# A graph layer on one core: look-ups in the order of their PSUM banks, masks bank by bank, layer one in two parts

## The reference

```python
h = maximum(layernorm(x), 0)                    # x: 12500 nodes x 32
e = concatenate([h[src], h[dst], edge_attr])    # 400000 edges, sorted by dst
hid = relu(e @ W1 + b1)                         # 96 -> 64
v = hid @ W2 + b2                               # 64 -> 32
out = x + maximum(segment_max(v, dst, 12500), h)
```

## Time and profile before

| what | us |
| --- | --- |
| measured, median of 3 runs | 3184.88 |
| lowest and highest | 3180.12 and 3187.65 |
| span of the profiled execution | 4798.8 |
| TensorE busy in it | 3796.5 |
| GpSimd busy in it | 2386.6 |
| ScalarE busy in it | 2192.4 |
| VectorE busy in it | 2178.1 |

### The profile page before, as it was taken

The page is one execution under the profiler, slowest core; times in us unless marked ns, Lnnn a source line. Parts: engine busy times, 40 slices in busy tenths (PEclk is TensorE's granted clock), DMA queues, the critical chain, the costliest instruction groups (busy, mean ns, idle before and its releaser), DMA issues.

```text
span 4798.8 us, 56874 instructions
## 1 busy us (share of the span) xinstructions
PE 3796.5 (79%) x19778; PEld 2547.3 (53%) x19778; DVE 2178.1 (45%) x2474; ACT 2192.4 (46%) x2555; POOL 2386.6 (50%) x2523
## 2 busy tenths in 40 slices
PE   5858788778878877877887788778877887778787
PEld 3536455555555545555555555555555555555465
DVE  4211554445444444544444455444444454445356
ACT  2214454445444444544444445444544454445355
POOL 6653455555455455455545555555455555554310
PEclk8979888888778888888887888888888888888798
DMA  8700222222222222222222222222222222222112
GB/s 255 279 10 25 70 80 88 92 85 61 57 68 63 56 66 69 56 61 68 68 55 63 68 65 61 60 69 68 56 63 68 69 61 56 68 68 68 46 55 56
DMA packets 200553, 350.32 MB, mean 73 GB/s; under 512 B 73791, under 2 KB 124251, under 8 KB 200117
## 3 DMA queue, kind: packets, MB, share of 16 engines
q1 hardware_dynamic: 116638, 303.65, 18.4%
q0 software_dynamic: 80448, 41.33, 6.2%
q10 hardware_dynamic: 3332, 4.01, 0.3%
HBM read 240.36 MB, written 119.78 MB: 75 GB/s over the span
## 4 chain that ended last, share of the span: by engine, by line
PE 60%; issue 19%; another core or an unknown queue 10%; DVE 8%; ACT 2%; DMA 0%; DVEq 0%; ACTq 0%; SPq 0%
PE ps_rows L938 38%; PE ps_layers L968 8%; PE ps_layers L963 5%; DVE onehot L1250 3%; PE ps_layers L918 2%; PE ps_layers L953 2%; PE ps_layers L912 2%; DVE max_t L1318 2%; PE ps_layers L957 2%; PE ps_layers L1006 1%; DVE src_t L1285 1%; DVE rows_in L1323 1%; ACT onehot L852 0%; DVE dst_t L1305 0%
## 5 line engine op out<-in xcount | busy, mean ns | idle before, releaser
L664 POOL DMA_INDIRECT src_in<-h_dram,src_ix x2269 | 2147.7, 947 | 1951.5 <-PE ps_rows L938 976.5
L938 PE MATMUL ps_rows<-onehot,table 128*128 128x512 f32 x9898 | 2553.2, 418 | 109.0 <-issue 89.3
L938 PEld LDWEIGHTS ps_rows<-onehot,table 128*128 128x128 f32 x9898 | 1986.6, 203 | 728.8 <-issue 292.8
L852 ACT ACTIVATE onehot<-distance 128x1024 fp32r<-128x1024 bf16 x909 | 905.0, 1049 | 855.0 <-PE ps_rows L938 607.3
L847 ACT ACTIVATE distance<-picks,below_column 128x1024 bf16<-128x1024 int16 x909 | 985.1, 1139 | 0.7 <-DMA picks<-picks_dram 0.7
L838 ACT ACTIVATE hid<-ps_layers,b_col 128x512 f32<-128x512 f32 (+1 forms) x404 | 241.6, 680 | 1407.9 <-remote 912.0
L1300 DVE STREAM_TRANSPOSE ps_layers<-rows_in 128x512 f32<-128x512 f32 x202 | 133.3, 706 | 1561.3 <-ACT hid L838 1561.2
L968 PE MATMUL ps_layers<-picked_rows,w_src 128*64 128x128 f32 x1552 | 399.9, 390 | 550.1 <-issue 545.7
L1250 DVE SCALAR_TENSOR_TENSOR onehot<-picks,column,ps_layers 128x1024 fp32r<-128x1024 int16 x404 | 499.8, 1258 | 310.2 <-PE ps_rows L938 164.7
L968 PEld LDWEIGHTS ps_layers<-picked_rows,w_src 128*64 128x64 f32 x1552 | 188.8, 180 | 784.9 <-issue 782.2
L1318 DVE TENSOR_TENSOR_SCAN max_t<-mask_in,max_t,ps_layers 128x512 f32<-128x512 bf16 x196 | 249.0, 1271 | 337.2 <-remote 331.4
(11 more groups left out here) (145 smaller groups left out, 1283.1 us busy)
## 6 DMA issues: line engine op xcount, KB each, us to landing
picks<-picks_dram SPq DMA_DIRECT2D x101, 512.0 KB
first_rows<-hid SPq DMA_DIRECT2D x100, 500.0 KB
rows_in<-in_edge_attr_dram SPq DMA_DIRECT2D x96, 512.0 KB
rows_in<-first_rows SPq DMA_DIRECT2D x96, 512.0 KB
run_max<-rows_in SPq DMA_DIRECT2D x96, 512.0 KB
src_in<-h_dram,src_ix POOLq DMA_INDIRECT x2269
mask_in<-mask_dram SPq DMA_DIRECT2D x96, 256.0 KB
h_dram<-h_sb ACTq DMA_DIRECT2D x4, 392.0 KB, 5.9
```

The lines of the kernel that those rows point to most:

```text
L664: pool.indirect_dma_start(out=src_in[:, slot, g, r, :], out_offset=None, in_=rows[:, :], in_offset=bass.IndirectOffsetOnAxis(ap=src_ix[:, ...
L852: nc.scalar.activation(onehot[:, RING_AT[c] + BY_DVE[c] + k, :, :].rearrange("p g w -> p (g w)"), distance[:, k, :], ACT.Relu, bias=1.0, s ...
L938: mm = nc.tensor.matmul(ps_rows[g][side][:, 0:WIDE], table[:, i * SIDES + side, part, :], onehot[:, RING_AT[c] + t, g, :], start=(i + part ...
```

## The change

Four things are written otherwise; the arithmetic is the same.

1. The look-ups of a chunk go bank by bank, in the order (side 1, g 0), (side 1, g 1), (side 0, g 0), (side 0, g 1), where before each tile went over sides and parts with g innermost. A new semaphore `banks_summed` counts the first three banks of the last chunk, and `tiles_used` goes up at the ends of banks (by 3 at the end of the last chunk).
2. Each of the four operations of `mask_rows` waits for its own bank, and each bank of chunk 0 waits for the mask that read it.
3. Layer one stands in two parts: edges and dst rows, two banks of chunk 0, gathered and picked rows, the other two banks of chunk 0. Layer two moves behind chunk 1.
4. VectorE's order in a pair is now: one-hot of chunk 0, masks, turn_edges, turn_src, (a wait for `hid` of pair j), one-hot of chunk 2, fill_dst, find_side, one-hot of chunk 3, find_max.

```diff
-                    for side in range(SIDES if i < WIDE_TILES else 1):
-                        last_tile = TILES - 1 if side == 0 else WIDE_TILES - 1
-                        parts = PARTS if i < WIDE_TILES else 1
-                        for part in range(parts):
-                            for g in range(2):
-                                mm = nc.tensor.matmul(ps_rows[g][side][:, 0:WIDE], table[:, i * SIDES + side, part, :],
+                    if side and i >= WIDE_TILES:
+                        continue
+                    last_tile = WIDE_TILES - 1 if side else TILES - 1
+                    parts = PARTS if i < WIDE_TILES else 1
+                    for part in range(parts):
+                        mm = nc.tensor.matmul(ps_rows[g][side][:, 0:WIDE], table[:, i * SIDES + side, part, :],
...
+                if c == CHUNKS - 1:
+                    if n < len(BANKS) - 1:
+                        mm.then_inc(banks_summed, 1)
+                    else:
+                        mm.then_inc(tiles_used, CHUNK[c])
+                elif n >= len(BANKS) - CHUNK[c]:
                     mm.then_inc(tiles_used, 1)
...
-                    layer_one(j, slot, True, short)
-                look_up(j + 2, slot, 0)
+                    layer_edges(j, slot)
+                    layer_dst(j, slot)
+                    look_up_bank(j + 2, 0, 0)
+                    look_up_bank(j + 2, 0, 1)
+                    layer_src(j, short)
+                    layer_picks(j, slot, short)
+                    look_up_bank(j + 2, 0, 2)
+                    look_up_bank(j + 2, 0, 3)
+                look_up(j + 2, 1)
...
-                dve.wait_ge(tiles_used, j * TILES + WIDE_TILES)
                 for g in range(2):
+                    dve.wait_ge(banks_summed, j * (len(BANKS) - 1) + (g + 1))
...
+                turn_src(j + 1, (k + 1) % (2 * AHEAD), turn + (k + 1) // (2 * AHEAD))
+                dve.wait_ge(hid_made, j * A + A)
+                dve.sem_inc(layer_passed, 1)
+                one_hot(j + 2, slot, 2)
                 fill_dst(j + 1, 1 - slot, of_next * D + D, of_next * D + D, j + 1)
-                one_hot(j + 2, slot, 2)
+                find_side(j + 2, slot)
+                one_hot(j + 2, slot, 3)
                 find_max(j, slot, stored)
-                one_hot(j + 2, slot, 3)
-                find_side(j + 2, slot)
-                turn_src(j + 1, (k + 1) % (2 * AHEAD), turn + (k + 1) // (2 * AHEAD))
```

More of the change, by code:

```diff
@@ L922, in _, with look_up_bank @@
             pe.wait_ge(table_step, TABLE_STEPS)
[L924 to L927, removed]
+            def look_up_bank(j, c, n):
+                side, g = BANKS[n]
+                if c == 0 and (not isinstance(j, int) or j > 0):
+                    if side:
+                        pe.wait_ge(second_side, j * 2 - 1 + g)
+                    else:
+                        pe.wait_ge(rows_masked, j * MASKS - 1 + g)
+                if n == 0 and BY_DVE[c]:
@@ new lines, in look_up_bank @@
+                    last_tile = WIDE_TILES - 1 if side else TILES - 1
+                    parts = PARTS if i < WIDE_TILES else 1
+                    for part in range(parts):
+                        mm = nc.tensor.matmul(ps_rows[g][side][:, 0:WIDE], table[:, i * SIDES + side, part, :],
+                                              onehot[:, RING_AT[c] + t, g, :],
+                                              start=(i + part == 0), stop=(i == last_tile and part == parts - 1))
+                if c == CHUNKS - 1:
+                    if n < len(BANKS) - 1:
+                        mm.then_inc(banks_summed, 1)
+                    else:
+                        mm.then_inc(tiles_used, CHUNK[c])
+                elif n >= len(BANKS) - CHUNK[c]:
@@ L941, in look_up, with layer_edges @@
                     mm.then_inc(tiles_used, 1)
-            def layer_one(j, slot, ahead=True, short=False):
+            def look_up(j, c):
+                for n in range(len(BANKS)):
+                    look_up_bank(j, c, n)
+            def layer_edges(j, slot):
                 wait(pe, max_scanned, j * 2)
-                pe.wait_ge(onehot_made, j * DVE_ALL + (2 * DVE_ALL + 1 if ahead else (PAIRS - j) * DVE_ALL))
-                pe.wait_ge(side_found, j + 2 if ahead else PAIRS)
-                pe.wait_ge(dst_filled, j * 2 + 2 if ahead else PAIRS * 2)
+                pe.wait_ge(onehot_made, j * DVE_ALL + (2 * DVE_ALL + 1))
+                pe.wait_ge(side_found, j + 2)
+                pe.wait_ge(dst_filled, j * 2 + 2)
@@ L1019, in pair @@
                     layer_two(j)
-                for c in range(1, CHUNKS):
-                    look_up(j + 2, slot, c)
+                for c in range(2, CHUNKS):
+                    look_up(j + 2, c)
             for j in range(2):
                 for c in range(CHUNKS):
-                    look_up(j, j, c)
+                    look_up(j, c)
             for j in range(2):
@@ L1291, in turn_edges, with fill_dst @@
                     V.transpose(of_half(ea_t[:, slot, :, :], h), ea_in[:, slot, h, :, :]).then_inc(ea_turned, 1)
-            def fill_dst(j, slot, loaded, masks, through, columns=(BLK, BLK), before=(BLK, BLK)):
+            def fill_dst(j, slot, loaded, masks, through, columns=(BLK, BLK), before=(BLK, BLK), made=True):
                 dve.wait_ge(first_loaded[slot], loaded)
@@ L1410, in _ @@
             turn_edges(0, 0, D)
-            fill_dst(0, 0, D, D, 0)
+            fill_dst(0, 0, D, D, 0, made=False)
             def pair(j, k, turn, stored, before_last=False):
@@ L1443, in tail_pair @@
                     dve.wait_ge(side_found, PAIRS)
[L1444 to L1446 removed]
+                    fill_dst(j + 2, slot, moved_up_to(j + 2), ((j + 2) // 2 + 1) * D, j + 1, columns_of(j + 2), columns_of(j + 1), made=False)
             for k in range(2 * AHEAD):
```

38 lines of the change are left out of this document (25 added, 13 removed).

## The result

The changed kernel takes 3199.87 us (3198.63 to 3201.24), the kernel before 3186.27 us in the same comparison: a ratio of 1.0045, 95% interval 1.0032 to 1.0059. So it is slower by 14 us. The forecast of 3186 us, "within 0.2%", was not what came. The time lies inside the range, but that is luck in part: the range had been widened upwards for rival B, in which TensorE sets the time, and what came is not B, as the experiments show.

A forecast was written before the change was run, and what follows sets the result against it. GpSimd's issuing of gathers was taken to bound the kernel, 30.04 against TensorE's 27.28 us a pair. The terms 3184.9 + 0 + 1 (the end) + 0 gave 3186 us, range 3170 to 3228 for 8 in 10.

The forecast's parts named there:

- rival B: Whole kernel: TensorE sets the time, split runs add 33 us; 3218 us (3205 to 3228), chance 0.24.
- What bounds the kernel: Main loop: GpSimd's issuing of gathers sets the time, 30.04 us a pair against TensorE's 27.28.
- Its sum for GpSimd: Rebuilt unprofiled time: 352 to the loop's start, 2812 for 2247 gathers, 12 behind the last; 3176 us.
- TensorE's own sum: Rebuilt unprofiled time by TensorE: start at 359, pairs 2619, the end 115.5; 3094 us, 91 below the median.
- 96 pairs of 27.28: TensorE's main loop: every pair at the undisturbed pace of 27.28 us, 2619 us in all.
- The split: TensorE's pair: one more look-up run and layer restart, 0.34 us (0.2 to 0.44), 33 us in all, covered by gathers.
- The bank order: TensorE's look-ups, now in runs into one bank: no change taken from 0.227 us each.
- a lead of 91: TensorE against the measured time: its sum of 3094 us stood 91 us below the median.
- The end: Behind the last gathers: longer VectorE latency paid once, 17.5 + 96.0 = 113.5 against GpSimd's 113.9; 0 to 3 us, 1 taken.
- T + 17.5: Last pair: its edges start 17.5 us after the last gathers land, instead of some 5.
- C: Rival, program's end: latency behind the last landing is dearer, masks or find_max 5 to 10 us late; 3190 to 3195, chance 0.08.
- The start: First gathers of the loop: earlier turn_src can save between 0 and 10 us; 0 taken.

The follow-up runs named there:

- second profile of before: The kernel before, unchanged, run once more for a profile without the first profile's gaps; span 3180.4 us, against 4798.8 us in the first.
- Experiment 6: The kernel before with one gather of rows in 24 left out, the last of each pair from 7 to 95; 3152.31 us, 0.9907 of before.
- experiment 1: The kernel before with VectorE's new order alone; look-ups, masks and layer one as before; 3198.36 us, 1.0051 of before.
- the last run of experiment 5: The changed kernel with turn_src behind find_max in pairs 90 to 95 and SLACK 13 for 6; 3182.55 us, 1.0002 of before.
- experiment 4: The changed kernel with turn_src behind find_max in all pairs, 3203.51 us; then also with SLACK 13 for 6, 3203.84 us.
- the run of experiment 3: The changed kernel with turn_src alone moved behind find_max in the last 15 pairs (from 84 on); 3189.90 us, 1.0022 of before.

## Why the prediction was right and wrong

**What bounds the kernel: right.** Its sum for GpSimd was 352 + 2812 + 12 = 3176. In the second profile of before the loop's first gather starts at 357.3, the last of all at 3168.6, 2811 later, and 11.8 us follow. That 2812 met 2811 so closely is luck: the step is 1.2486 us and not 1.2515, 6.5 us less over 2247 steps, and 5.14 of waiting for the stores and 2.0 of gaps, which the sum did not have, make up for it. 1.25 us from gather to gather holds in the profile that isn't stretched, with the same 0.30 between windows that the prediction's sentence on the Trainium skill (Perfetto Trace Analysis, "Per-instruction lifecycle: what the profiler-reported window actually captures") rested on. Experiment 6 shows the rest.

**TensorE's own sum: mis-sized.** It was 3094; experiment 6, in which TensorE ends last, has 3152. The term that failed is "96 pairs of 27.28". In experiment 6, and in the kernel before too, the first 13 pairs took 388 us and not 355; in that stretch one-hots wait for the loads of `picks`, as ScalarE's row of before has it:

```profile
ACT distance L847 <- DMA picks<-picks_dram: 72.1, 11, 8.7
```

Another 14 us of experiment 6 are in pairs 27, 28, 41, 42, 55, 69 and 70, that is every 14 pairs, the length of VectorE's loop.

The longest stretch of before, pairs 82 and 83, is not TensorE's own. TensorE's rows, VectorE's fill_dst in the same pair, and SyncE's waits from 2640 to 2700 us:

```profile
2683.30 11.15 PE L938 MATMUL ps_rows<-onehot,table 128*128 128x512 f32 x42 [11.91 <-DVE onehot L1250]
...
2700.26 2.02 PE L953 MATMUL ps_layers<-ea_t,w_edge 32*64 32x512 f32 x16 [5.81 <-DVE onehot L1250]
```

```profile
2678.12 1.32 DVE L1300 STREAM_TRANSPOSE ps_layers<-rows_in 128x512 f32<-128x512 f32 x2 [20.06 <-DMA mask_in<-mask_dram]
```

```profile
SPq L607 <- DMA src_in<-h_dram,src_ix: 38.3, 2, 23.3
```

SyncE waits at line 607 for GpSimd's gathers to land before it loads the next indices, and the loads of `mask_in` and `picks` that stand behind this in its queue come late. So GpSimd's lateness reaches TensorE by this way as well. The two pairs take 75.4 us before and 64.4 after; in experiment 6 SyncE never waits there, and pair 82 takes 27.3.

**The split: right.** 0.34 us a pair was predicted (0.2 to 0.44), 27.69 - 27.27 = 0.42 came. The bank order costs nothing, 0.227 us a look-up in either. turn_src starts 7.7 us into a pair (7.6 predicted), the masks 1.5 us ahead of the pair's end (about 1). It was hidden, as forecast: experiment 1, without any of it, is as slow. But it was hidden by less than the prediction thought. 97 times 0.42 are 41 us, well under a lead of 91 and more than one of 30. Where pair 96 begins in experiment 6, and in the last run of experiment 5, whose TensorE waits for no late landing either:

```profile
3030.49 1.11 PE L955 MATMUL ps_layers<-ea_t,w_edge 32*64 32x512 f32 x16
```

```profile
3064.99 1.11 PE L969 MATMUL ps_layers<-ea_t,w_edge 32*64 32x512 f32 x16
```

In these two profiles TensorE's own work comes 34.5 us later with the change, about where GpSimd's landings had put it before (3065.70). So the lead is used up, and a kernel with the end set right is level with the one before and no faster.

**The end: this step failed.** The prediction sized the delay well, 17.5 us in place of 5, or 12.5; 12.3 came. It then said that this is paid behind the *last* landing, T of pair 96, so that pair 96's edges stand at T + 17.5, and that GpSimd's 113.9 us of maxima cover it to 0.4 us. But pair 96 is short: its 13 gathers take 16.3 us, less than a pair of TensorE. So the chain runs from the landing of pair 95, through 15.8 us of VectorE's queue and the whole of pair 95, 29.3 us, to pair 96: its edges start at 3082.61, where T + 17.5 would be some 3068 (the last gather of rows starts at 3048.18 and lands 2 to 3 us later). Those 14 to 15 us are nearly all of the wait of 15.29. What lies behind, 96.0 us, was right (95.6). Of the rivals C is the nearest, "the latency at the end is dearer", with a chance of 0.08. It did not give this reason, though: it thought of masks or find_max being late behind the last landing, not of the landing before it. Its 5 to 10 us came as 10.2, the difference between the two waits (15.29 and 5.14), and with the later gathers, below, the time is above its 3190 to 3195.

**The start: the sign was wrong.** Earlier turn_src was to save between 0 and 10 us there, and 0 was taken. The loop's first gather did start 0.7 us earlier (356.5 against 357.3), but TensorE's first 13 pairs took 398.6 us in place of 388.3, so `tiles_used` came later, and gaps opened between the gathers of pairs 13 to 19: over the whole loop 6.1 us in place of 2.0. The prediction named `tiles_used` as coming later within a pair and gave it no price. Experiment 1 has these gaps too, with the old look-up order (7.6 us), and 399.8 us for the first 13 pairs; so VectorE's order opens them, not the banks. Which of its moves does is open. In experiment 4, with turn_src back behind find_max, no gap of note ends with a look-up any more, but larger ones end with turn_src (14.1 us in all), so it does not tell.

**Open.** Of the 7.0 us by which the last gather of rows is late, 4.1 are these gaps, and 0.7 came back at the start. The other 3.5 are a step of 1.2502 us in place of 1.2486, over 2148 steps. The same loop has 1.2486 in the run of experiment 3 (whose gaps, 8.6 us, make up its later last gather by themselves), so this belongs to the execution and not to the change; what sets it is not known.

## What to carry to other kernels

When a waiting instruction is moved forward on an in-order engine, the loop may not notice and the end will: follow the chain from each of the last landings, not from the last one alone, since a short last item makes the one before it the head. An order that is right in the loop can be wrong in its last few iterations, and these can have their own. A wait can also pass through a third queue: here loads that stood behind a waiting one in SyncE's queue handed GpSimd's lateness on to TensorE. And where an engine is taken as the bound, its lead over the next one should be measured (leave out some of its work and see how far the time falls) before another engine's work is called hidden.

## What the runs showed of the hardware

After 3.94 us of waiting, TensorE ran the next layer at half speed. The rows before, TensorE's timeline and the busy time of the stretch that it begins and of one right behind it:

```profile
1165.79 2.01 PE L953 MATMUL ps_layers<-ea_t,w_edge 32*64 32x512 f32 x16 [3.94 <-DVE onehot L1250]
```

```profile
1165.79:1170.72 4.93, 4.93 (x49) 1.55 (x49) 4.14 (x6) 0.06 (x1) 3.78 (x4) 0.50 0.49 160
1171.74:1179.26 7.52, 7.52 (x34) 5.93 (x32) 3.88 (x4) 3.96 (x6) 5.69 (x7) 1.00 0.18 47
```

The granted clock is 0.50 there, the 1.2 GHz level, and 1.00 again some 5 us on; line 953 took 2.01 us in place of 1.11. The other surprise is the first profile itself: the same, unchanged kernel had a span of 4798.8 us in one profiled execution and 3180.4 in another.
